# A linear-attention and gated-FFN layer on eight cores: other order of DMAs in the first tile, later residual rows, other order of the last output projections

## Chip, cores and metric

One Trainium2 chip, all 8 cores, each core running the same program on its own two of the sixteen sequences. The metric is the device time in microseconds of the slowest core; lower is better.

## What is computed

For each sequence x (2048 tokens of 1024 floats), after a layer norm `xn`:

```python
s = attn(xn)       # five mixed inputs x + (x_prev - x) * mu, products with r_w, k_w, v_w, g_w,
                   # a decay from tanh(.. @ w_w1.T) @ w_w2.T + w_b2, a recurrence over chunks of 32
                   # tokens with 4 heads (state 128 x 256), group norm per head, times silu(g), @ o_w.T
h = silu(xn @ wg.T) * (xn @ wu.T)        # wg, wu: 3072 x 1024, int32 weights / 127
g = silu(h @ wd.T)                       # wd: 1024 x 3072, int32 weights / 127
x = x + s * g
```

## The kernel before

**Tiles.** A core walks over its 4096 tokens in `N_MT` = 8 tiles of 512 tokens (`it` = 0 to 7); the tiles of one sequence hand the state `sb_S` and the last token on. A tile has `NST` = 4 rows of 128 tokens (`t`). All weights pass through SBUF in every tile, in slots: four for the gate and up weights (`sb_gu`, 24 steps `hc`, 512 KB each in bf16), four for a ring of eight attention weights (`sb_ring`: r, k, v0, v1, g0, g1, o0, o1, 1 MB each), and one half of the down weights in four groups `g` of six chunks (`sb_wd`, 768 KB each).

**Casts, stores and loads.** GpSimd's queue casts weights from their 4-byte originals (`w_gu`, `w_fd`, `w_g` and so on) to bf16 while they travel (`cast_gu`, `cast_ring`, `cast_wd`). At the last cast of a weight SyncE's queue stores the bf16 form to DRAM (`keep_gu`, `keep_ring`, `keep_wd`), and from the next tile on ScalarE's queue loads this form (`load_gu`, `load_ring`, `load_wd`). Down weights are cast in tile 0 alone, ring slots r and k in tiles 0 and 1, the others up to tile 3. A cast or load into a slot waits for the store of what lay in it (`k_wd`, `k_ring`, `k_gu`).

**A tile's stages.** TensorE's order is written out by hand (lines 1348 to 1501). Gate steps `gate_up(it, hc)` (16 matmuls each, lines 1180 to 1188) alternate with the mixing products, then r, k, v and g. Then for each row `t`: `out_and_kv` (recurrence), the transposes of the next tile's `xn`, `scores(t + 1)`, and two of eight down units. Unit `u` is row `u % 4` of half `u // 4`, so units 0 to 3 use the first half of the down weights and units 4 to 7 the second; pass t of this loop runs units 2t and 2t + 1, each as `down_first` (12 chunks, line 1300) and `down_second` (12 chunks, line 1311). The second half is loaded into the space of the first while units 3 and following run: group g as soon as unit 3 has used group g (`t_wd`, `t_D`). Transposes of the gated output (`og_transpose`, line 1325), its copy to `sb_ogT` by ScalarE (`copy_ogT`, line 687) and the output projection (`out_proj`, line 1339) follow two rows later; those of the third and fourth row (t = 2, 3) stand behind the last unit, between the first two gate steps of the next tile. The last tile has no next tile, so there they stand alone.

**The other engines.** VectorE's `output(it, t)` (line 1040) multiplies the projection by silu(down) and adds the residual row; `shift_and_xin0` (line 838) makes the first mixed input, and clears `sb_stash`, `sb_S` and `sb_Sb` at a sequence's start. ScalarE's `silu_down` (line 667) frees a down unit's bank.

**Order of the queues around the change.** A wait in a queue holds what is behind it. SyncE, tile 0: x rows for the next tile, stores of the first down half (line 388), residual rows one and two, x rows three and four, stores of o0 and o1, of the next tile's gate weights and r and k, stores of the second down half, residual rows three and four (after the last scores, line 332), output stores. GpSimd, tile 0: the first tile's casts by hand (lines 511 to 568), o0, o1, then the next tile's gate weights and ring slots r and k (line 602), and after the group norm of t = 1 the second down half (line 610). ScalarE: the second half is loaded at t = 1 and the first half for the next tile at t = 3 (line 794).

```python
                if t % 2 == 1:
                    for g in range(3):
                        load_wd(it + t // 2, 1 - t // 2, g)
                silu_down(it, 2 * t + 1)
                if t % 2 == 1:
                    load_wd(it + t // 2, 1 - t // 2, 3)
```

Of the kernel before, what the change touches and what calls it, by code (L numbers as in the profile page):

```python
# [102 lines left out]
N_MT = SPC * NMT  # L103
NGU = 4
# [38 lines left out]
def build_program():  # L143
# [165 lines left out]

    def d_unit(u):  # L310
        return (u % 4, u // 4)

    def sync_program(e):
# [52 lines left out]
        for it in range(N_MT):  # L366
            nxt = it + 1 < N_MT
            if it == 0:
                for hc in range(4):
                    keep_gu(0, hc)  # L370
            for hc in range(4, 10):
# [16 lines left out]
            for g in range(4):  # L388
                keep_wd(it, 0, g)
# [5 lines left out]
            keep_ring(it, 6)  # L395
            keep_ring(it, 7)
            if nxt:
                for hc in range(4):
                    keep_gu(it + 1, hc)
                keep_ring(it + 1, 0)  # L400
                keep_ring(it + 1, 1)
            for g in range(4):
                keep_wd(it, 1, g)
            load_res(it, 2)
            load_res(it, 3)
            for t in range(NST):
                store_out(it, t)
        for t in range(NST):
            e.wait_ge(d_out[t], 16 * N_MT)

    def pool_program(e):
# [157 lines left out]
        for it in range(N_MT):  # L569
# [28 lines left out]
            if nxt:  # L598
# [3 lines left out]
                for j in (0, 1):  # L602
                    cast_ring(it + 1, j, 0)
                    cast_ring(it + 1, j, 1)
            for t in range(NST):
# [3 lines left out]
                if t == 1:  # L609
                    for g in range(4):  # L610
                        cast_wd(it, 1, g, 0)
                        cast_wd(it, 1, g, 1)

    def scalar_program(e):
# [110 lines left out]
        for it in range(N_MT):  # L725
# [14 lines left out]
            for hc in range(6, 10):  # L740
                silu_gu(it, hc)
            if it:
# [43 lines left out]
            for t in range(NST):  # L786
# [11 lines left out]
                if t % 2 == 1:  # L798
                    load_wd(it + t // 2, 1 - t // 2, 3)
            copy_ogT(it, 2)  # L800
            if nxt:
                silu_gu(it + 1, 0)
            copy_ogT(it, 3)
            if nxt:
                silu_gu(it + 1, 1)

    def vector_program(e):
# [30 lines left out]
        def shift_and_xin0(it):  # L838
            if it % NMT == 0:
                if it:  # L840
                    e.wait_ge(t_ow, 4 * it)
# [198 lines left out]
        def output(it, t):  # L1040
            if t >= 2:
                e.drain()
            e.wait_ge(t_O, 4 * it + t + 1)
            e.wait_ge(a_D, 8 * it + 5 + t)
            for half in range(2):
                i = e.tensor_tensor(  # L1046
                    out=sg_sb[:, 512 * half:512 * half + 512],
                    in0=P_o[half][:],
# [12 lines left out]
        e.memset(sb_G64[:].rearrange("p b c -> p (b c)"), 1.0)  # L1061
        e.drain().then_inc(v_init, 1)
# [13 lines left out]
        ln_xnt(0, 0)  # L1076
        first_stat(2)
        ln_xnt(0, 1)
# [451 lines left out]
```

## Time and profile before

| | us |
|---|---|
| median of 3 runs (1811.79 to 1815.5) | 1813.17 |
| the profiled execution | 1834.1 |
| its span, slowest core (5) | 1832.5 |
| its span, fastest core (0) | 1803.2 |
| TensorE busy, core 5 | 1725.5 (94%) |
| VectorE, ScalarE, GpSimd busy | 1093.3, 476.9, 164.1 |

The profiled execution is another one than the timed ones and is taken on its slowest core. Busy time is time in which the engine executes; the waits of an engine are its idle stretches with what ended them. A queue's share is the time of its packets over 16 DMA engines and the span. MB count the bytes at the destination.

### The profile page before, as it was taken

To read this page: it belongs to the slowest core of one execution; us is meant where nothing else is said; L and a number is where in the kernel's file an instruction comes from. 1 tells how busy PE (TensorE), PEld (TensorE's weight loads), DVE (VectorE), ACT (ScalarE), POOL (GpSimd) and SP (SyncE) were. 2 spreads that over 40 slices of the span, in tenths; PEclk is the share of its full clock that TensorE was granted. 3 is DMA by queue.
4 is the path that set the end of the run, shared out by engine and by line. 5 is a ranking of instruction groups with operands and counts; after the bars stand their busy time and mean duration, and the time that the engine had idled before them with its cause. 6 is when DMAs were issued, how large, how long until landed. Compare 5 with 4: busy or idle time off the path is not lost.

```text
span 1832.5 us, 26740 instructions; the slowest of 8 cores (1803.2 to 1832.5 us)
## 1 busy us (share of the span) xinstructions
PE 1725.5 (94%) x9248; PEld 796.3 (43%) x9248; DVE 1093.3 (60%) x1887; ACT 476.9 (26%) x802; POOL 164.1 (9%) x354
## 2 busy tenths in 40 slices
PE   4999759999999999999999999999999999999997
PEld 2434424344444454444544444444454445444443
DVE  5554617465764847646664657656576485764654
ACT  0133201143211432125311332114321143212411
POOL 2211301101101011000100001000010001000000
PEclk9999869999999999999999999999999999999999
DMA  8999987997489954896545355543537454464231
GB/s 160 159 168 213 221 199 170 163 175 177 155 199 214 214 138 151 214 211 189 168 143 154 123 173 161 175 147 122 189 116 218 135 161 128 147 195 133 92 106 57
DMA packets 71506, 299.27 MB, mean 163 GB/s; under 512 B 8463, under 2 KB 8912, under 8 KB 64720
## 3 DMA queue, kind: packets, MB, share of 16 engines
q10 hardware_dynamic: 31680, 153.11, 26.9%
q0 software_dynamic: 19680, 66.76, 23.9%
q1 hardware_dynamic: 20016, 77.69, 12.8%
q8 instruction: 78, 1.28, 0.3%
q14 instruction: 52, 0.43, 0.1%
HBM read 320.25 MB, written 44.04 MB: 199 GB/s over the span
## 4 chain that ended last, share of the span: by engine, by line
PE 83%; DMA 11%; DVE 2%; issue 1%; DVEq 1%; ACT 1%; POOL 0%; ACTq 0%; SPq 0%; POOLq 0%
PE PB L1181 17%; PE PB L1186 16%; PE PB L1311 8%; PE PB L1300 7%; PE PB L1449 6%; PE PB L1473 6%; PE PB L1339 6%; DMA sb_wd<-kept_wd 4%; DMA sb_gu<-w_gu 4%; PE PB L1209 3%; PE PB L1392 3%; PE PB L1409 3%; DMA sb_wd<-w_fd 2%; PE PB L1359 1%; DMA sb_xin<-x 1%
## 5 line engine op out<-in xcount | busy, mean ns | idle before, releaser
L1181 PE MATMUL PB<-sb_xnT,sb_gu 128*128 128x512 bf16 x1536 | 369.0, 384 | 12.4 <-DMA sb_gu<-w_gu 9.7
L1186 PE MATMUL PB<-sb_xnT,sb_gu 128*128 128x512 bf16 x1536 | 364.8, 380 | 0.0
L814 DVE SCALAR_TENSOR_TENSOR sb_hall<-PB,sb_scr 128x512 bf16<-128x512 f32 x192 | 131.2, 687 | 333.2 <-ACT sb_scr L663 332.9
L663 ACT ACTIVATE sb_scr<-PB 128x512 bf16<-128x512 f32 x192 | 113.8, 597 | 613.7 <-PE PB L1186 607.5
L1181 PEld LDWEIGHTS PB<-sb_xnT,sb_gu 128*128 128x128 bf16 x1536 | 142.6, 98 | 210.7 <-issue 58.7
L1186 PEld LDWEIGHTS PB<-sb_xnT,sb_gu 128*128 128x128 bf16 x1536 | 151.0, 98 | 183.5 <-issue 4.1
L882 DVE SCALAR_TENSOR_TENSOR sb_xin<-PB,sb_xb,sb_dT 128x512 bf16<-128x512 f32 x320 | 217.3, 741 | 0.0
L1311 PE MATMUL PB<-sb_wd,sb_hall 128*128 128x512 bf16 x768 | 181.3, 385 | 30.2 <-DMA sb_wd<-kept_wd 21.9
L1300 PE MATMUL PB<-sb_wd,sb_hall 128*128 128x512 bf16 x768 | 180.3, 383 | 23.7 <-DMA sb_wd<-w_fd 21.0
L1311 PEld LDWEIGHTS PB<-sb_wd,sb_hall 128*128 128x128 bf16 x768 | 74.3, 98 | 122.3 <-issue 38.6
L672 ACT ACTIVATE sb_wc<-PB 128x512 bf16<-128x512 f32 x64 | 38.2, 597 | 338.8 <-PE PB L1311 338.8
L1339 PE MATMUL PB<-sb_ring,sb_ogT 128*128 128x512 bf16 x512 | 117.6, 383 | 3.7 <-ACT sb_ogT L687 3.3
L1300 PEld LDWEIGHTS PB<-sb_wd,sb_hall 128*128 128x128 bf16 x768 | 72.0, 98 | 107.6 <-issue 30.1
L1473 PE MATMUL PB<-sb_ring,sb_xin 128*128 128x512 bf16 x512 | 113.1, 379 | 0.0
L994 DVE SCALAR_TENSOR_TENSOR sb_S<-sb_S,sb_GS,PB 128x256 f32<-128x256 f32 x128 | 53.0, 476 | 99.5 <-PE PB L1288 99.5
L1449 PE MATMUL PB<-sb_ring,sb_xin 128*128 128x512 bf16 x512 | 111.8, 379 | 0.0
L888 DVE TENSOR_TENSOR sb_xin<-sb_xin,sb_xnT 128x2048 bf16<-128x2048 bf16 x80 | 98.0, 1225 | 7.3
L1046 DVE TENSOR_TENSOR sb_x<-PB,sb_wc 128x512 f32<-128x512 f32 x64 | 41.1, 684 | 76.5 <-PE PB L1339 74.9
L1025 DVE TENSOR_SCALAR sb_dT<-sb_dT,sb_mv,sb_rs 128x256 bf16<-128x256 f32 x128 | 44.2, 408 | 59.5 <-POOL sb_rs L508 59.5
L1339 PEld LDWEIGHTS PB<-sb_ring,sb_ogT 128*128 128x128 bf16 x512 | 50.2, 99 | 63.7 <-issue 6.9
L485 POOL TENSOR_SCALAR sb_lr<-sb_ls 128x1 f32<-128x1 f32 x28 | 12.0, 430 | 724.1 <-ACT sb_scr L654 724.0
L1449 PEld LDWEIGHTS PB<-sb_ring,sb_xin 128*128 128x128 bf16 x512 | 50.0, 98 | 60.5
(147 smaller groups left out, 1773.1 us busy)
## 6 DMA issues: line engine op xcount, KB each, us to landing
sb_gu<-kept_gu ACTq DMA_DIRECT2D x120, 512.0 KB, 4.1
sb_ring<-kept_ring ACTq DMA_DIRECT2D x44, 1024.0 KB, 7.4
sb_wd<-kept_wd ACTq DMA_DIRECT2D x56, 768.0 KB, 7.4
sb_gu<-w_gu POOLq DMA_DIRECT2D x72, 512.0 KB, 11.8
sb_xin<-x SPq DMA_DIRECT2D x48, 512.0 KB, 9.3
kept_gu<-sb_gu SPq DMA_DIRECT2D x24, 512.0 KB, 7.8
sb_ring<-w_g POOLq DMA_DIRECT2D x16, 512.0 KB, 11.9
kept_ring<-sb_ring SPq DMA_DIRECT2D x8, 1024.0 KB, 14.1
```

Source lines behind the costliest of these rows:

```text
L663: e.activation(out=sb_scr[:, p, :], in_=GB[p][:], func=AF.Silu, bias=0.0, scale=INV127).then_inc(a_silu, 1)
L814: e.scalar_tensor_tensor(out=sb_hall[:, hc, :], in0=UB[p][:], scalar=INV127, in1=sb_scr[:, p, :], op0=ALU.mult, op1=ALU.mult).then_inc(v_h, 1)
L882: e.scalar_tensor_tensor(out=sb_xin[:, p, c, :], in0=PM[j][:], scalar=sb_xb[:, n, c:c + 1], in1=sb_dT[:, c, :], op0=ALU.add, op1=ALU.mult) ...
L888: e.tensor_tensor(out=sb_xin[:, p, c0:c0 + 4, :], in0=sb_xin[:, p, c0:c0 + 4, :], in1=sb_xnT[:, c0:c0 + 4, :], op=ALU.add).then_inc(v_xin, 1)
L1181: e.matmul(GB[p][:], sb_gu[:, sl, 0, c, :], sb_xnT[:, c, :], start=(c == 0), stop=(c == NC - 1))
L1186: i = e.matmul(UB[p][:], sb_gu[:, sl, 1, c, :], sb_xnT[:, c, :], start=(c == 0), stop=(c == NC - 1))
L1209: i = e.matmul(PM[c % 4][:], sb_wx2[32 * n:32 * n + 32, 0, c * 128:(c + 1) * 128], sb_x5[32 * n:32 * n + 32, 0, :], start=True, stop=True, ...
L1300: i = e.matmul(PB[u % 2][:], sb_hall[:, hc, 128 * t:128 * t + 128], sb_wd[:, hc, :], start=(hc == 0), stop=False, skip_group_check=True)
L1311: i = e.matmul(PB[u % 2][:], sb_hall[:, hc, 128 * t:128 * t + 128], sb_wd[:, hc, :], start=False, stop=(hc == NHC - 1), skip_group_check=True)
L1339: i = e.matmul(P_o[half][:], sb_ogT[:, c, :], sb_ring[:, 2 + half, c, :], start=(c == 0), stop=(c == NC - 1), skip_group_check=True)
L1449: i = e.matmul(PM[t][:], sb_xin[:, 1, c, 128 * t:128 * t + 128], sb_ring[:, 2 + half, c, :], start=(c == 0), stop=(c == NC - 1))
L1473: i = e.matmul(PM[t][:], sb_xin[:, 0, c, 128 * t:128 * t + 128], sb_ring[:, half, c, :], start=(c == 0), stop=(c == NC - 1))
```

## The change

The order of SyncE's queue is changed (stores of ring slots r and k at the start of their tile, stores of down weights later, residual rows three and four after down unit 4, first output store ahead of the stores of o0 and o1). GpSimd casts ring slots r and k for tile 1 after the group norm of t = 2, and issues `w_x0` one cast later. ScalarE loads the next first down half at gate steps 6 to 9 of the tile that uses it. VectorE clears the state before it waits for the first rows, and normalises the second row before it takes statistics of the third. In the last tile the projection of the third row (t = 2) goes to banks 2 and 3 between the halves of down unit 7, the transposes of the third and fourth row stand around it, and the fourth row is projected, multiplied, added and stored in halves.

```diff
+LAST = N_MT - 1
+    def out_banks(it, t):
+        return PB[2:4] if it == LAST and t == 2 else P_o
 # load_res, t >= 2
-                e.wait_ge(t_mt, 4 * (it + 1))
+                e.wait_ge(t_D, 8 * it + 5)
 # store_out
+            if it == LAST and t == 3:
+                e.dma_start(out_d[s, ts, 0:512], res[t][:, 0:512]
+                            ).then_inc(d_out[t], 16)
+                e.wait_ge(v_out, 4 * it + t + 2)
+                e.dma_start(out_d[s, ts, 512:1024], res[t][:, 512:1024]
+                            ).then_inc(d_out[t], 16)
+                return
 # sync_program, start of a tile
+            keep_ring(it, 0)
+            keep_ring(it, 1)
...
-            for g in range(4):
-                keep_wd(it, 0, g)
             load_res(it, 0)
             load_res(it, 1)
             if nxt:
                 load_x(it + 1, 2)
                 load_x(it + 1, 3)
-            keep_ring(it, 6)
-            keep_ring(it, 7)
+            for g in range(4):
+                keep_wd(it, 0, g)
             if nxt:
                 for hc in range(4):
                     keep_gu(it + 1, hc)
-                keep_ring(it + 1, 0)
-                keep_ring(it + 1, 1)
+            load_res(it, 2)
+            load_res(it, 3)
+            store_out(it, 0)
+            keep_ring(it, 6)
+            keep_ring(it, 7)
             for g in range(4):
                 keep_wd(it, 1, g)
-            load_res(it, 2)
-            load_res(it, 3)
-            for t in range(NST):
+            for t in range(1, NST):
                 store_out(it, t)
 # pool_program
         ln_rstd(0, 0)
-        e.dma_start(sb_wx0[:], wdr["w_x0"]).then_inc(d_x0w, 16)
         ln_rstd(0, 1)
         cast_gu(0, 1)
+        e.dma_start(sb_wx0[:], wdr["w_x0"]).then_inc(d_x0w, 16)
...
                 for hc in range(0 if it else 2, 4):
                     cast_gu(it + 1, hc)
-                for j in (0, 1):
-                    cast_ring(it + 1, j, 0)
-                    cast_ring(it + 1, j, 1)
             for t in range(NST):
...
+                if t == 2 and nxt:
+                    for j in (0, 1):
+                        cast_ring(it + 1, j, 0)
+                        cast_ring(it + 1, j, 1)
 # scalar_program
             for hc in range(6, 10):
                 silu_gu(it, hc)
+                load_wd(it, 0, hc - 6)
...
                 if t < 3:
                     copy_ksT(it, t + 1)
-                if t % 2 == 1:
+                elif not nxt:
+                    copy_ogT(it, 2)
+                    copy_ogT(it, 3)
+                if t == 1:
                     for g in range(3):
-                        load_wd(it + t // 2, 1 - t // 2, g)
+                        load_wd(it, 1, g)
 # vector_program: the memsets of sb_stash, sb_S, sb_Sb for it == 0 stand ahead of v_init
         ln_xnt(0, 0)
+        ln_xnt(0, 1)
         first_stat(2)
-        ln_xnt(0, 1)
 # output, last tile, t == 3
+                e.wait_ge(a_D, 8 * it + 8)
+                e.wait_ge(d_res[t], 16 * (it + 1))
+                for half in range(2):
+                    hs = slice(512 * half, 512 * half + 512)
+                    e.wait_ge(t_O, 4 * it + t + 1 + half)
+                    e.tensor_tensor(out=sg_sb[:, hs], in0=po[half][:], in1=gff[...], op=ALU.mult)
+                    e.drain()
+                    e.tensor_tensor(out=res[t][:, hs], in0=res[t][:, hs],
+                                    in1=sg_sb[:, hs], op=ALU.add).then_inc(v_out, 1)
 # tensor_program, row loop
+                if t == 3 and not nxt:
+                    og_transpose(it, 2)
                 down_first(it, 2 * t + 1)
+                if t == 3 and not nxt:
+                    out_proj(it, 2)
+                    og_transpose(it, 3)
                 down_second(it, 2 * t + 1)
```

## Rows read from the trace of the kernel before

**Rows 1.** Head of the page.

```profile
span 1832.5 us, 26740 instructions; the slowest of 8 cores (1803.2 to 1832.5 us)
```

**Rows 2.** TensorE's waits, core 5: waited for, us in total, times, longest.

```profile
PE PB L1311 <- DMA sb_wd<-kept_wd: 21.9, 13, 2.8
PE PB L1300 <- DMA sb_wd<-w_fd: 21.0, 2, 18.5
...
PE PB L1311 <- DMA sb_wd<-w_fd: 8.2, 2, 6.1
```

**Rows 3.** TensorE's waits, core 0.

```profile
PE PB L1311 <- DMA sb_wd<-kept_wd: 9.0, 9, 1.7
```

**Rows 4.** Chain that ended last, first tile: start us, us, what.

```profile
217.94 41.43 DMA sb_wd<-w_fd
```

**Rows 5.** Page, DMA queues: packets, MB, share of 16 engines.

```profile
q10 hardware_dynamic: 31680, 153.11, 26.9%
q0 software_dynamic: 19680, 66.76, 23.9%
q1 hardware_dynamic: 20016, 77.69, 12.8%
```

**Rows 6.** Windows: us, busy PE PEld DVE ACT POOL, PEclk, DMA share, GB/s.

```profile
220.00:230.00 10.00, 1.33 (x28) 0.89 (x22) 7.84 (x22) 0.00 (x0) 2.16 (x3) 0.50 1.03 232
270.00:280.00 10.00, 10.00 (x66) 5.62 (x65) 6.30 (x18) 2.22 (x3) 0.26 (x2) 1.00 0.13 52
570.00:580.00 10.00, 10.00 (x46) 3.95 (x44) 7.07 (x11) 1.89 (x4) 0.86 (x2) 1.00 1.05 170
```

**Rows 7.** Timeline of the SyncE and GpSimd queues, tile 0: start us, us, what.

```profile
148.15 23.32 SPq L358 DMA_DIRECT2D kept_wd<-sb_wd  x4
...
188.12 14.27 SPq L325 DMA_DIRECT2D sb_xin<-x  x2
...
187.89 0.54 POOL L430 DMA_DIRECT2D sb_ring<-w_k  x1
...
213.98 0.69 POOL L467 DMA_DIRECT2D sb_wd<-w_fd  x1
```

**Rows 8.** Timeline of TensorE, tile 0 (in brackets: idle us before, what ended it).

```profile
166.19 2.18 PE L1181 MATMUL PB<-sb_xnT,sb_gu 128*128 128x512 bf16 x7 [3.74 <-DMA sb_gu<-w_gu]
...
239.81 2.72 PE L1300 MATMUL PB<-sb_wd,sb_hall 128*128 128x512 bf16 x6 [18.48 <-DMA sb_wd<-w_fd]
```

**Rows 9.** TensorE in tiles 1, 2; cast issued at 563.9; page, median gate load.

```profile
334.93 3.33 PE L1181 MATMUL PB<-sb_xnT,sb_gu 128*128 128x512 bf16 x8 [2.28 <-DMA sb_gu<-w_gu]
...
580.87 1.46 PE L1181 MATMUL PB<-sb_xnT,sb_gu 128*128 128x512 bf16 x6
...
sb_gu<-w_gu POOLq DMA_DIRECT2D x1, 512.0 KB, 15.2
...
sb_gu<-kept_gu ACTq DMA_DIRECT2D x120, 512.0 KB, 4.1
```

**Rows 10.** Chain, and timeline of SyncE, in tile 4's fourth stage.

```profile
1126.30 11.30 DMA sb_wd<-kept_wd
...
1129.22 0.33 SPq L333 DMA_DIRECT2D sb_ke<-x  x1
```

**Rows 11.** Timeline of VectorE and TensorE at the start.

```profile
27.83 0.91 DVE L843 MEMSET sb_S<- 128x1024 f32 x1 [0.16 <-issue]
...
37.27 1.89 PE L1356 MATMUL PB<-sb_xin,sb_wx 128*128 128x512 bf16 x8 [1.00 <-DVE sb_xin L859]
```

**Rows 12.** Timeline of TensorE and VectorE at the end.

```profile
1817.37 3.61 PE L1339 MATMUL PB<-sb_ring,sb_ogT 128*128 128x512 bf16 x16 [1.64 <-ACT sb_ogT L687]
...
1823.06 3.61 PE L1339 MATMUL PB<-sb_ring,sb_ogT 128*128 128x512 bf16 x16 [1.64 <-ACT sb_ogT L687]
...
1826.85 1.29 DVE L1046 TENSOR_TENSOR sb_x<-PB,sb_wc 128x512 f32<-128x512 f32 x2 [3.02 <-PE PB L1339]
1828.30 1.22 DVE L1054 TENSOR_TENSOR sb_k<-sb_k,sb_x 128x1024 f32<-128x1024 f32 x1 [0.16 <-issue]
```

More of the change, by code:

```diff
@@ L793, in scalar_program @@
                     copy_ksT(it, t + 1)
-                if t % 2 == 1:
+                elif not nxt:
+                    copy_ogT(it, 2)
+                    copy_ogT(it, 3)
+                if t == 1:
                     for g in range(3):
-                        load_wd(it + t // 2, 1 - t // 2, g)
+                        load_wd(it, 1, g)
                 silu_down(it, 2 * t + 1)
-                if t % 2 == 1:
-                    load_wd(it + t // 2, 1 - t // 2, 3)
-            copy_ogT(it, 2)
+                if t == 1:
+                    load_wd(it, 1, 3)
             if nxt:
+                copy_ogT(it, 2)
                 silu_gu(it + 1, 0)
-            copy_ogT(it, 3)
-            if nxt:
+                copy_ogT(it, 3)
                 silu_gu(it + 1, 1)
@@ L838, in shift_and_xin0 @@
         def shift_and_xin0(it):
-            if it % NMT == 0:
-                if it:
-                    e.wait_ge(t_ow, 4 * it)
+            if it and it % NMT == 0:
+                e.wait_ge(t_ow, 4 * it)
                 e.memset(sb_stash[:], 0.0)
@@ L1042, in output @@
                 e.drain()
+            po = out_banks(it, t)
+            if it == LAST and t == 3:
+                e.wait_ge(a_D, 8 * it + 8)
[3 more added lines that the diff above has]
+                    e.wait_ge(t_O, 4 * it + t + 1 + half)
+                    e.tensor_tensor(
+                        out=sg_sb[:, hs], in0=po[half][:],
+                        in1=gff[:, t * D + 512 * half:t * D + 512 * half + 512],
+                        op=ALU.mult)
+                    e.drain()
+                    e.tensor_tensor(out=res[t][:, hs], in0=res[t][:, hs],
+                                    in1=sg_sb[:, hs], op=ALU.add
+                                    ).then_inc(v_out, 1)
+                return
             e.wait_ge(t_O, 4 * it + t + 1)
@@ L1047, in output @@
                     out=sg_sb[:, 512 * half:512 * half + 512],
-                    in0=P_o[half][:],
+                    in0=po[half][:],
                     in1=gff[:, t * D + 512 * half:t * D + 512 * half + 512],
@@ L1061, in vector_program @@
         e.memset(sb_G64[:].rearrange("p b c -> p (b c)"), 1.0)
+        e.memset(sb_stash[:], 0.0)
+        e.memset(sb_S[:].rearrange("p h v -> p (h v)"), 0.0)
+        e.memset(sb_Sb[:].rearrange("p h v -> p (h v)"), 0.0)
         e.drain().then_inc(v_init, 1)
@@ L1321, in og_transpose @@
             e.wait_ge(v_S, 4 * it + s + 1)
-            if t == 3:
-                e.wait_ge(a_ogT, 4 * it + 3)
+            if t == 3 or (it == LAST and t == 2):
+                e.wait_ge(a_ogT, 4 * it + t)
             for c in range(NC):
@@ L1329, in out_proj @@
         def out_proj(it, t):
+            po = out_banks(it, t)
             e.wait_ge(a_ogT, 4 * it + t + 1)
             e.wait_ge(v_o, 4 * it + min(t + 2, 3) + 1)
-            if t == 3:
-                e.wait_ge(v_sg, 4 * it + 3)
-            elif t == 2:
+            if it == LAST and t == 2:
+                e.wait_ge(a_ksT, 4 * it + 4)
+                e.wait_ge(v_sel, 4 * it + 4)
+            elif it == LAST and t == 3:
                 e.wait_ge(v_sg, 4 * it + 2)
+            elif t >= 2:
+                e.wait_ge(v_sg, 4 * it + t)
             for half in range(2):
@@ L1338, in out_proj @@
                 for c in range(NC):
-                    i = e.matmul(P_o[half][:], sb_ogT[:, c, :],
+                    i = e.matmul(po[half][:], sb_ogT[:, c, :],
                                  sb_ring[:, 2 + half, c, :], start=(c == 0),
                                  stop=(c == NC - 1), skip_group_check=True)
+                if it == LAST and t == 3 and half == 0:
+                    i.then_inc(t_O, 1)
             i.then_inc(t_O, 1)
```

9 lines of the change are left out of this document (4 added, 5 removed).

## The prediction

> **What bounds the kernel now.** I read the page's head first: the profiled execution spans 1832.5 us on its slowest core, core 5, and 1803.2 us on its fastest [rows 1]. TensorE works for 94% of it, so only its idle time can be won. The waits of TensorE [rows 2] name that idle time. Two groups matter here: 21.0 + 8.2 us for casts of the down weights from `w_fd`, four waits that all lie in the first tile; 21.9 us for `kept_wd` loads, 13 waits over the later tiles. The chain of waits [rows 4] shows the first group as one transfer: the last cast of the second half of the down weights is issued at 217.94 and lands 41.4 us later, at 259.4. TensorE was ready for the first quarter of these weights at 239.81 - 18.48 = 221.3 [rows 8].
>
> Why it lands so late is in three more views. The queue rows [rows 5] give each queue's own rate: q0 (GpSimd's casts) moved 66.76 MB in 23.9% of 1832.5 us, 152 GB/s; q10 (ScalarE's loads) 310 GB/s; q1 (SyncE) 331 GB/s. By these a 512 KB cast costs 3.4 us of all 16 DMA engines, a 384 KB cast 2.6, a 768 KB load 2.5, a 1 MB store 3.2, a 512 KB residual row 1.6. The windows [rows 6] show the DMA full (1.03) at 220 to 230 with TensorE at half clock, and almost empty (0.13) at 270 to 280. The timeline [rows 7] shows that the casts of ring slots r and k, which only the next tile's r and k products need, are issued up to 187.89, ahead of the down casts (from 213.98) in the same queue.
>
> **The change part by part**, on core 5's profiled time, then on the median.
>
> *A, the start.* The three memsets (0.91 us for sb_S, as much for sb_Sb) leave VectorE's path to the first x0 product. TensorE waited 1.00 us there and before that worked on gate_up [rows 11], so 1.0 us is all they give. VectorE does them while it waits for the first x rows. The swapped first rows (`ln_xnt(0,1)`, `w_x0` behind a gate cast) end at the same landing of row four: 0. The displaced `w_x0` stands behind one more cast, 3.4 us, and is used at 37.27 at the earliest; both casts are issued in the first 15 us, so nobody waits.
>
> *B, gate cast 23 of the first tile.* It is waited for 3.74 us at 166.19 [rows 8]. Beside it SyncE's stores of the first down half run from 148.15 [rows 7], 2.4 us of DMA each. The change puts them behind the residual and x loads, near 202. Two of them, 4.7 us, leave the time of this cast: gain 3.7, bounds 0 and 3.7.
>
> *C, the second down half in the first tile.* The four ring casts (13.8 us of q0) go behind it. SyncE's o0 and o1 stores go behind the first output store; the four first-half stores come in their place, 9.5 us from 202. GpSimd's down casts wait for these stores, but by 214 they should have landed, since q0 holds nothing else then. Eight casts by 2.6 us and the time to landing (4.1 us for a 512 KB load whose transfer is 1.7 [rows 9], so 2.4) give 213.98 + 20.7 + 2.4 = 237.1, against 259.4: 22.3. The floor for the gain is the case that the stores hold q0 up for their whole 9.5 us: 13. The ceiling is the whole wait, 29.2. I take 23, since x row three, which GpSimd's queue waits for ahead of the casts, lands earlier too, and 1 us more because the matmuls behind it come back to full clock earlier (a group of six took 2.72 us behind the wait, where the clock of [rows 6] is half). The ring casts then run in the empty stretch near 250 to 280. Sum 24. Some 10 us of wait remain.
>
> *D, residual rows three and four.* They are issued at 1129.22, in the middle of the `kept_wd` loads whose last takes 11.3 us from 1126.30 [rows 10]. Now they wait for unit 4, which needs the last of these loads. Two rows are 3.2 us of DMA. As they land little later than the weights, about half of that was spent before them: I take 1.8 us a tile, 12.6 over seven tiles; bounds 0 and 21.9 [rows 2]. Their user is `output(it,2)`, three units later. Behind them in SyncE's in-order queue stands the first output store, ready only after the first out projection, which itself follows unit 4; so it is not held up. Of the Trainium skill, "DMA: Bandwidth & Descriptors" (Queues, rings and completion order) bears on this: each DMA engine takes turns between the queues that have work, a packet at a time. By that rule SyncE's rows take a full turn from the moment they are issued, and with 3.2 us a tile the sum would be 9.8 us larger on core 5. The issue times [rows 10] agree with turns being shared; no row shows how they are shared, so 1.8 stays.
>
> *E and F, the price.* The loads of the first down half for tile it+1 go from the end of tile it to gate steps 6 to 9 of tile it+1: 4 x 2.5 = 9.9 us of q10 at another place. Where they were, the gate weights had long landed. Where they go, tile 1 has waited for a cast already (2.28 us at 334.93) [rows 9], so it has no reserve. The loads also share with the stores of ring slots r and k (6.3 us), moved behind the output stores. Against this, the queue is emptier by the same 9.9 us before step 4. I take 4 us lost; bounds 0 and 10. In tile 2 the DMA is full (1.05 at 570 to 580 [rows 6]). The cast of step 13, issued at 563.9, lands 15.2 us later at 579.1, TensorE takes it at 580.87 [rows 9]: 1.8 us of reserve. Up to 9.9 - 1.8 = 8 can be lost; SyncE's stores carry a part: 5 taken. From tile 3 on a gate load takes 4.1 us [rows 9] and is issued three steps ahead. Six matmuls take 1.46 us [rows 9], so a step of 16 takes at least 3.4 and three 10.2: a 2.5 us neighbour is hidden, 0.
>
> *G, the end.* Two copies of ogT are waited for (1.64 us each) at 1817.37 and 1823.06 [rows 12]. The products of rows three and four now stand around the last down unit, whose matmuls cover both copies: 3.3. VectorE works in halves, so behind the last matmul there are one multiply (0.65) and half an add (0.6 to 0.7) and not 1.29 + 1.22: 1.3. The last store is half as large; with other small gaps 0.4. Sum 5, bounds 3 and 6. Row three's product moves to banks 2 and 3, whose last readers (the select and the copy of ksT for t = 3) stand before unit 6: no wait.
>
> Sum for core 5: 1.0 + 3.7 + 24 + 12.6 - 4 - 5 + 5 = 37.3, from 1834.1 us (span and 1.6 around it) to 1796.8. The median of the runs is 1813.17, 21 us under the profiled one, so its slowest core has shorter waits; core 0 shows 9.0 us where core 5 has 21.9 [rows 3]. C, B and G are alike on both cores; D I cut by the mean of the two, to 8.8. That leaves 33.5: **1780 us**.
>
> **The rivals.**
> (1) *The gates starve in tiles 1 and 2.* The moved loads meet a full DMA, and both tiles lose 8 to 10 us, with C at its floor of 13: gain 1 + 3.7 + 13 + 8.8 - 18 + 5 = 13.5, 1800 us. For it: the reserves of [rows 9]. Against: before step 4 there is less in the queues. The turns of the Trainium skill's page ("DMA: Bandwidth & Descriptors", the same section) speak for it as well: a cast that TensorE waits for gets no more turns than a load with time to spare. Chance 0.11.
> (2) *Slower.* ScalarE's queue is in order, so each gate load now stands behind a down load. If that starved the gates in all seven tiles by the full 9.9 us, 69 us would be lost against 42.5 won (the sum without E and F): 1813 + 27 = 1840. It decides from 6.1 us a tile. Against: 4.1 us to landing within 10.2 of lead leaves 6.1 for a 2.5 us neighbour. Chance 0.03.
> (3) *C does not come.* SyncE's in-order queue holds the first-half stores behind x row four, which waits for VectorE; if they land only at 230, GpSimd's down casts start there and land at 253.1: C is 6.3, the gain 1 + 3.7 + 6.3 + 8.8 - 9 + 5 = 15.8, 1797 us. Against: that x load was issued by 188.12 + 14.27 = 202.4 before [rows 7]. Chance 0.05.
> (4) *No price.* Tiles 1 and 2 hide the loads and C reaches 27: gain 45.5, 1768. It belongs to my forecast's range. Chance 0.16, and 0.65 for the forecast itself.
>
> **How the numbers follow.** A measurement of this kernel tells about 0.2%, 3.6 us, from no change. Faster by more: forecast, (4), (1) and (3), less a little for several mishaps together: 0.95. Slower by more 0.03, between 0.02. The range takes in (4) and most of C's and D's bounds on the fast side, 1764, and reaches short of the cases at 1797 and 1800 on the other, 1796.
>
> **What would show it.** C: the last `w_fd` landing near 232 to 237 after about 5 us of shift, and the w_fd waits down from 29 to about 10 us; (3) is right if the first down cast of the second half is issued after 220. B: no wait at gate cast 23. D: `kept_wd` waits at most half as long. E, F: new `sb_gu` waits at steps 8 to 13 of tiles 1 and 2, together near 9 us more than before; if they exceed 18, (1) is right, and if tiles 4 to 7 show any, (2). G: no wait for sb_ogT in the last 20 us. I am wrong if the time is above 1796, or if C gives under 15 us.

## The result, and the profile after

The changed kernel takes 1809.3 us (median of 20 runs) where the kernel before takes 1820.93 in as many: a ratio of 0.9914, 95% interval 0.9889 to 0.9938. Timed again later on another occasion (the run after_again, below) the ratio was 0.9883, 0.9844 to 0.9922. Eight of the changed kernel's 20 executions ran with a lower granted clock on one die (0.81 to 0.96) and took 1855 us or more, so the ratios are of the others and are not the quotient of the medians. So it is faster, by 16 to 21 us by the two ratios; the forecast was 1780 us, 33 us less than before, with a range from 1764 to 1796. The direction held and the size did not. Of the distance between 1780 and 1809.3, 7.8 us lies in the starting point: the forecast began at 1813.17, the median of three runs, where 20 runs give 1820.93.

The head of the page of the changed kernel, its rows of TensorE and of the DMA queues (packets, MB, share of 16 engines):

```profile
span 1799.9 us, 26572 instructions; the slowest of 8 cores (1783.3 to 1799.9 us)
...
PE 1711.7 (95%) x9073; PEld 795.4 (44%) x9248; DVE 1094.0 (61%) x1888; ACT 476.6 (26%) x802; POOL 164.2 (9%) x354
...
q10 hardware_dynamic: 31680, 153.11, 24.1%
q0 software_dynamic: 19680, 66.76, 23.4%
q1 hardware_dynamic: 20160, 77.69, 12.2%
```

The profiled executions differ more than the timed medians: 1834.1 us before, 1801.44 after. That of before [rows 1] is a long one among its runs (the 20 timed ones go from 1811.79 to 1837.18), so rows are not to be subtracted total from total, but stage by stage, over all eight cores. TensorE's waits in the profile after, core 4, the slowest (waited for, us in total, times, longest):

```profile
PE PB L1215 <- DMA sb_gu<-w_gu: 16.6, 7, 5.8
...
PE PB L1334 <- DMA sb_wd<-w_fd: 10.2, 2, 7.2
PE PB L1215 <- DVE sb_hall L830: 5.1, 2, 4.3
PE PB L1345 <- DMA sb_wd<-kept_wd: 4.8, 9, 1.2
...
PE PB L1345 <- DMA sb_wd<-w_fd: 3.8, 2, 2.7
```

Lines 1334, 1345 and 1215 are `down_first`, `down_second` and `gate_up`, lines 1300, 1311 and 1181 before. The waits for `w_fd` fell from 29.2 us [rows 2] to 14.0, those for `kept_wd` in `down_second` from 21.9 to 4.8. (Summed over both lines and as the mean of all eight cores they fell from 30.5 to 14.0 and from 15.2 to 4.7.) A new first row stands over them: 16.6 us for gate casts, on the mean of the cores 17.9 where it was 9.2. Of the 5.1 us of `sb_hall`, 4.3 are one wait in tile 2 of another kind, shown below.

**The stages.** Each tile is cut at two products that every core makes in the same place: the x0 product at its start, and the g product that ends its gate steps. "Front" is x0 to g, "back" is g to the next x0 (in the last tile, to the end). The table is worked out from the start times of these matmuls in the timeline; mean over the eight cores of one profiled execution each, in us. All kernels of the experiments stand in it, and the text comes back to it. The front of tiles 3 to 7 is 122.0 to 122.2 in every one.

```
kernel           to x0  front0 back0  front1  front2  backs 1-6  last back  span: mean, slowest
before            36.7  132.7  130.9  126.1   122.0    564.7       95.1     1817.9  1832.5
after             35.4  128.8  110.8  136.1   129.8    554.0       87.3     1792.0  1799.9
after_again       35.1  129.1  111.5  137.2   129.6    553.4       87.6     1793.2  1801.7
e1_loads_back     35.1  129.3  117.1  132.1   122.2    559.5       89.0     1794.0  1799.3
e2_loads_late     35.6  128.5  111.0  133.9   122.2    555.6       88.3     1785.0  1794.8
e3_rings_early    35.2  129.7  110.8  134.0   130.9    554.8       87.8     1793.0  1801.9
e4_only_res       36.2  133.7  130.4  125.6   122.1    555.2       92.9     1805.8  1813.6
e5_only_tail      36.1  132.3  130.5  126.7   122.2    559.1       88.1     1804.8  1813.2
e6_only_queues    36.4  128.8  123.9  125.7   122.2    560.6       94.4     1801.9  1813.5
e8_queues_late    36.5  128.6  113.8  125.4   122.2    556.3       94.2     1787.0  1793.9
e7_late_early     35.2  129.7  110.4  128.3   122.0    553.8       87.3     1776.5  1782.3
e7_again          34.9  129.3  111.3  128.5   122.6    552.3       87.3     1776.2  1783.4
```

Read the first two lines: every stage won, the back of tile 0 by 20 us, except two. The fronts of tiles 1 and 2 lost 10.0 and 7.8 us. That is where most of the missing gain went. On the mean of the cores TensorE's idle time in these two stretches grew by 7.4 and 5.6 us, nearly all at gate steps; the rest, 2.6 and 2.1, is longer busy time, since the matmuls behind a wait run slower (eight of them take 3.29 us at 315.95 below and 1.89 at 305.62; the granted clock was 0.53 from 316 to 319 us and 1.00 from 305.6 to 309). Its timeline in tile 1, core 4 (in brackets: idle us before, what ended it):

```profile
305.62 1.89 PE L1215 MATMUL PB<-sb_xnT,sb_gu 128*128 128x512 bf16 x8 [0.81 <-DVE sb_hall L830]
...
315.95 3.29 PE L1215 MATMUL PB<-sb_xnT,sb_gu 128*128 128x512 bf16 x8 [5.75 <-DMA sb_gu<-w_gu]
...
324.92 1.19 PE L1215 MATMUL PB<-sb_xnT,sb_gu 128*128 128x512 bf16 x4 [3.95 <-DMA sb_gu<-w_gu]
```

and in tile 2 on the same core:

```profile
558.34 3.27 PE L1215 MATMUL PB<-sb_xnT,sb_gu 128*128 128x512 bf16 x8 [1.89 <-DMA sb_gu<-w_gu]
566.10 1.89 PE L1215 MATMUL PB<-sb_xnT,sb_gu 128*128 128x512 bf16 x8 [1.80 <-DMA sb_gu<-w_gu]
573.97 2.34 PE L1215 MATMUL PB<-sb_xnT,sb_gu 128*128 128x512 bf16 x7 [4.25 <-DVE sb_hall L830]
```

The gaps are at steps 7, 8, 9 of tile 1 and 11, 12, 13 of tile 2. They do not all have one cause. The chain of waits (start us, us, what) runs through step 9 of tile 1:

```profile
281.74 0.33 SPq L349
...
282.17 0.40 SPq L362
...
282.65 1.05 SPq L362
...
283.80 20.01 DMA kept_gu<-sb_gu
...
304.33 20.34 DMA sb_gu<-w_gu
...
324.92 1.19 PE PB L1215 x4
```

From the bottom up: the matmuls of step 9 waited for their cast; that cast could be issued only at 304.33, because it overwrites the slot whose store (`kept_gu`) landed at 283.80 + 20.01 = 303.81; and this store was issued behind the last output store of tile 0 (line 349) and the two stores of ring slots r and k (line 362), which the change had moved right in front of it. Step 8 is another matter: its cast was issued at 295.59, when its slot was free, and took until 315.7 to land, beside the stores and, from 304.12 on, the first moved `kept_wd` load. So there were two suspects, the moved loads and the moved ring stores, and tile 1 alone could not tell which costs what.

The last gap of tile 2, 4.25 us at step 13, goes by yet another way. The chain there:

```profile
550.43 21.23 DMA kept_gu<-sb_gu
...
571.73 0.33 ACTq L635
...
572.21 0.61 ACT sb_scr L676
...
572.91 0.70 DVE sb_hall L830
...
573.97 2.34 PE PB L1215 x7
```

ScalarE's program has the load of gate weight 14 (line 635) behind the silu of step 10, and this load waits for the store of weight 10, which lay in the slot. The store took 21.2 us to land (9.1 in the kernel before on core 0 and 15.3 on core 4). The silu of step 11 stood behind that wait, VectorE's product behind the silu, and TensorE needed the bank for step 13. This wait (3.4 to 4.5 us) is on cores 0, 3, 4 and 6 alone: their front 2 is 132.6 to 133.6 us, that of the others 125.4 to 127.0. So nearly half of what tile 2 lost was not a late cast but ScalarE held by a slow store.

### The profile page after: what moved, and what is told of

The parts are those of the page before. It is cut to its first block, busy times and chain, and to the rows that moved or that the text cites. A ratio compares the mean times of both kernels' runs of the same rounds, so it can differ in the third digit from the quotient of the medians.

```text
span 1799.9 us, 26572 instructions; the slowest of 8 cores (1783.3 to 1799.9 us)
## 1 busy us (share of the span) xinstructions
PE 1711.7 (95%) x9073; PEld 795.4 (44%) x9248; DVE 1094.0 (61%) x1888; ACT 476.6 (26%) x802; POOL 164.2 (9%) x354
## 3 DMA queue, kind: packets, MB, share of 16 engines
q0 software_dynamic: 19680, 66.76, 23.4%
## 4 chain that ended last, share of the span: by engine, by line
PE 82%; DMA 12%; DVE 2%; issue 2%; DVEq 1%; ACT 1%; SPq 0%; POOL 0%; ACTq 0%; POOLq 0%
PE PB L1215 16%; PE PB L1220 16%; PE PB L1345 8%; PE PB L1334 7%; PE PB L1489 6%; PE PB L1513 6%; PE PB L1377 6%; DMA sb_gu<-w_gu 5%; PE PB L1449 3%; PE PB L1243 3%; DMA sb_wd<-kept_wd 3%; PE PB L1432 3%; DMA kept_gu<-sb_gu 2%; DMA sb_wd<-w_fd 1%; PE PB L1248 1%
## 5 line engine op out<-in xcount | busy, mean ns | idle before, releaser
L1215 PE MATMUL PB<-sb_xnT,sb_gu 128*128 128x512 bf16 x1489 | 365.1, 386 | 28.8 <-DMA sb_gu<-w_gu 16.6
L1334 PE MATMUL PB<-sb_wd,sb_hall 128*128 128x512 bf16 x730 | 173.5, 383 | 15.5 <-DMA sb_wd<-w_fd 10.2
L1345 PE MATMUL PB<-sb_wd,sb_hall 128*128 128x512 bf16 x752 | 179.0, 383 | 9.5 <-DMA sb_wd<-kept_wd 4.8
L685 ACT ACTIVATE sb_wc<-PB 128x512 bf16<-128x512 f32 x64 | 38.2, 597 | 315.6 <-PE PB L1345 315.6
L434 POOL DMA_DIRECT2D sb_gu<-w_gu x72 | 39.7, 552 | 400.2 <-PE PB L1220 354.7
```

The costliest lines, as they stand in the source:

```text
L1215: e.matmul(GB[p][:], sb_gu[:, sl, 0, c, :], sb_xnT[:, c, :], start=(c == 0), stop=(c == NC - 1))
L1334: i = e.matmul(PB[u % 2][:], sb_hall[:, hc, 128 * t:128 * t + 128], sb_wd[:, hc, :], start=(hc == 0), stop=False, skip_group_check=True)
L1345: i = e.matmul(PB[u % 2][:], sb_hall[:, hc, 128 * t:128 * t + 128], sb_wd[:, hc, :], start=False, stop=(hc == NHC - 1), skip_group_check=True)
```

## The experiments

All ratios are to runs of the kernel before on the same chip. That of e8 rests on two executions, those of e2 and e3 on three each, so these kernels are told apart by the stages and not by the ratios.

### Loads back, loads later, ring stores earlier: which of them starves the gates

**e1_loads_back**: the changed kernel with the loads of the next first down half where they were before.

```diff
             for hc in range(6, 10):
                 silu_gu(it, hc)
-                load_wd(it, 0, hc - 6)
...
-                if t == 1:
+                if t % 2 == 1:
                     for g in range(3):
-                        load_wd(it, 1, g)
+                        load_wd(it + t // 2, 1 - t // 2, g)
                 silu_down(it, 2 * t + 1)
-                if t == 1:
-                    load_wd(it, 1, 3)
+                if t % 2 == 1:
+                    load_wd(it + t // 2, 1 - t // 2, 3)
```

> The changed kernel with one part undone: the loads of the first down half for the next tile stand at t = 3 of the tile before again. In the changed kernel's profile the stretch from the x0 product to the g product is 135.8 us in tile 1 and 133.0 us in tile 2 on core 4 (before: 127.6 and 122.0 on core 5). Theory 1 (the moved loads starve the gate casts in tiles 1 and 2): both stretches fall by 7 to 11 us, to some 127 and 122, and the time is 0.7 to 1.0% under the changed kernel's ratio of 0.991, so 0.981 to 0.985 of before. Theory 2 (in tile 1 the stores of ring slots r and k, now at its start, are the cause): tile 2 falls to 122, tile 1 stays above 132; ratio 0.986. A wait of up to 5 us of ScalarE for the stores of the second down half may show at t = 3 of tile 0.

**e2_loads_late**: the changed kernel with these loads at gate steps 19 to 22, in tiles that have no shortage there.

```diff
-                load_wd(it, 0, hc - 6)
...
             for hc in range(19, 24):
                 silu_gu(it, hc)
+                if hc < 23:
+                    load_wd(it, 0, hc - 19)
```

> The changed kernel with the same four loads at gate steps 19 to 22 of the tile that uses them and not at steps 6 to 9; there the DMA was 0.25 to 0.83 busy in tile 1 of the kernel before. Theory 1: tile 1 and tile 2 stretches fall as without the move, to some 127 and 122 us, and no new wait comes at the first down unit, ratio 0.980 to 0.984. Theory 2: tile 1 stays above 132, ratio 0.986. If the late place collides with x rows and ring loads, waits for sb_wd at the first down unit show instead, 1 to 3 us a tile.

**e3_rings_early**: the changed kernel, loads as changed, but the stores of r and k of tile 1 at the end of tile 0's list instead of behind its output stores.

```diff
-            keep_ring(it, 0)
-            keep_ring(it, 1)
+            if it == 0:
+                keep_ring(it, 0)
+                keep_ring(it, 1)
...
             keep_ring(it, 6)
             keep_ring(it, 7)
+            if nxt:
+                keep_ring(it + 1, 0)
+                keep_ring(it + 1, 1)
```

> The changed kernel with one part undone: the stores of ring slots r and k are issued in tile 0 behind those of o0 and o1, not at the start of tile 1. Theory 2 (they delay the store of gate weight 5, and with it cast 9, and take 6.3 us of DMA from the casts of steps 6 to 8): the tile 1 stretch falls by 5 to 8 us, ratio 0.987. Theory 1: it falls by 0 to 3 us, since the loads at steps 6 to 9 remain; tile 2 stays as it is at 125 to 133; ratio 0.990 to 0.991.

Measured: e1 0.9872 (0.9837 to 0.9907), e2 0.9819 (0.9764 to 0.9873), e3 0.9881 (0.9838 to 0.9925).

**Tile 2 is settled**: its front is 122.2 in e1 and e2 and 130.9 in e3. The moved loads cost the whole 7.8 us there, by casts and by ScalarE's wait together, the ring stores nothing. **Tile 1 is not additive**: neither edit alone brings it back (132.1, 133.9, 134.0 against 136.1 to 137.2). Each suspect is enough to keep most of the loss. Core 5 of e2, where only the ring stores are left in the way, TensorE and then SyncE's queue:

```profile
298.47 1.89 PE L1216 MATMUL PB<-sb_xnT,sb_gu 128*128 128x512 bf16 x8 [0.65 <-DMA sb_gu<-w_gu]
305.95 3.16 PE L1216 MATMUL PB<-sb_xnT,sb_gu 128*128 128x512 bf16 x8 [2.91 <-DMA sb_gu<-w_gu]
314.05 1.89 PE L1216 MATMUL PB<-sb_xnT,sb_gu 128*128 128x512 bf16 x8 [2.24 <-DMA sb_gu<-w_gu]
321.76 3.15 PE L1216 MATMUL PB<-sb_xnT,sb_gu 128*128 128x512 bf16 x8 [4.10 <-DMA sb_gu<-w_gu]
```

```profile
279.28 0.33 SPq L349 DMA_DIRECT2D out<-sb_k  x1
279.71 1.36 SPq L362 DMA_DIRECT2D kept_ring<-sb_ring  x2
281.16 24.93 SPq L355 DMA_DIRECT2D kept_gu<-sb_gu  x2
```

Core 5 of e3, where only the loads are left:

```profile
309.07 1.89 PE L1219 MATMUL PB<-sb_xnT,sb_gu 128*128 128x512 bf16 x8 [0.75 <-DVE sb_hall L834]
320.51 3.57 PE L1219 MATMUL PB<-sb_xnT,sb_gu 128*128 128x512 bf16 x8 [7.83 <-DMA sb_gu<-w_gu]
```

The shapes differ. Ring stores give four small gaps at steps 6 to 9: the casts are slowed from the start (those of steps 7 and 8 take 17.2 and 20.7 us to land, 11.2 and 14.2 in e3), and cast 9 is issued late (303.06, after its `kept_gu` store landed 21.4 us after issue; in e3 that store takes 6.4 us and cast 9 goes out at 298.02). Loads give no more than 0.75 us before step 9 and one large gap there; its cast, issued on time, now takes 22.2 us. Both together overlap, since a late cast and a slow cast of the same step make one wait.

### Both at once

**e7_late_early**: both edits together, e2 and e3.

> Both undone at once: the loads of the first down half at gate steps 19 to 22, and the stores of ring slots r and k in tile 0. Each alone left the tile 1 stretch at 134 us (mean of cores), the changed kernel has 136, the kernel before 126. Theory 1+2 (two separate loads on a DMA that is full at steps 6 to 9; either alone is enough to starve the casts there): with both gone the stretch falls to 122 to 127 and the time to 0.972 to 0.978 of before. Rival (neither is the cause; tile 1 starts 25 us earlier against the rest of the DMA's work, for instance against its own chain of stored and recast gate weights): the stretch stays at 131 to 134, ratio 0.981 to 0.983.

Measured: **0.9737 (0.9694 to 0.9780)**, and once more beside the changed kernel on one chip:

> The changed kernel once more, to stand beside the next run on the same chip. If the ratio on record (0.991) is its own: 0.988 to 0.994. If the stages of the profiles are the whole story (20 us less than the kernel before on the mean of the cores): 0.987 to 0.990.

> The changed kernel with the loads at steps 19 to 22 and the stores of r and k for tile 1 at the end of tile 0, once more. By the stages of the profiles it is 15 us (0.9%) under the changed kernel, so 0.979 to 0.983 of the kernel before; by its first ratio (0.974) 30 us under it. Tile 1 from x0 to g 127 to 131 us, tile 2 122.0.

after_again 0.9883 (0.9844 to 0.9922); e7_again 0.9771 (0.9744 to 0.9798). This kernel beats both: over the changed one by 0.9771 / 0.9883 = 0.989, about 20 us, where the stages say 15.5 to 17. Its ratio came out a little below the 0.979 to 0.983 that the stages gave; the upper end of the interval, 0.9798, reaches into them. Front 1 is 128.3 and 128.5, just above the 122 to 127 first expected; front 2 is 122.0 and 122.6. So the two edits together give back 8.3 us of the 10.6 that tile 1 lost. Some 2.3 us remain against the kernels that leave tile 1 alone (125.4 to 126.7), and no run isolates their cause. Core 5 in tile 1:

```profile
307.96 1.89 PE L1220 MATMUL PB<-sb_xnT,sb_gu 128*128 128x512 bf16 x8 [0.39 <-DMA sb_gu<-w_gu]
...
315.40 3.57 PE L1220 MATMUL PB<-sb_xnT,sb_gu 128*128 128x512 bf16 x8 [3.83 <-DMA sb_gu<-w_gu]
```

and its chain there has no store left in it, a cast alone:

```profile
294.95 1.74 PE PB L1225 x8
...
297.28 17.88 DMA sb_gu<-w_gu
...
315.40 3.57 PE PB L1220 x8
```

The loads at steps 19 to 22 cost next to nothing in the table: front 2 is 122.0 to 122.6, and backs 1 to 6 are 553.8 and 552.3, as short as with the loads at steps 6 to 9.

### Parts of the change, alone, on the kernel before

**e4_only_res**: the kernel before with `load_res` for t >= 2 waiting for `t_D, 8 * it + 5`.

```diff
-                e.wait_ge(t_mt, 4 * (it + 1))
+                e.wait_ge(t_D, 8 * it + 5)
```

> The kernel before with one part of the change alone: residual rows three and four wait for down unit 4 and not for the last scores. My prediction's term D, 8.8 us on the median: ratio 0.995, kept_wd waits at the first unit of the second half down by half in each tile. Rival (the profiled execution of before was one with unusually long waits, and on a usual one the term is small): 2 to 4 us, ratio 0.998 to 0.999.

Measured 0.9958 (0.9928 to 0.9988): 7.7 us, with 2 to 13 in the interval. TensorE's waits on core 5 of this run, beside 21.9 us in the first group of [rows 2]:

```profile
PE PB L1311 <- DMA sb_wd<-kept_wd: 8.6, 12, 1.4
```

The stages correct this comparison. The kernels e5 and e6 keep the residual rows where they were, and their backs 1 to 6 sum to 559.1 and 560.6, not to the 564.7 of before. So about 5 us of what before's profile shows there belongs to that execution. Against the mean of the two, 559.9, the edit alone gives 4.7 us in six tiles, and 1.4 in the last (92.9 against 94.3, the mean of e6 and e8): 6.1. One run speaks against so much: e1 has this edit too, with the loads at t = 3 as here, and its backs 1 to 6 sum to 559.5, as in the kernels without it. The waits for `kept_wd` say the same (mean of the cores, us): 10.0 in e5, 11.9 in e6, 5.7 in e4, but 11.0 in e1. With one profiled execution of each the stages leave the size of this part open, from next to nothing to 6 us; the ratio says 2 to 13.

**e5_only_tail**: the kernel before with the changed last tile only, the same lines as in the change (`out_banks`, the copies, transposes and projections around unit 7, halves in `output` and `store_out`).

> The kernel before with the last tile's new order alone. My term G: 5 us, ratio 0.997, the last stretch of the profile some 5 us shorter (93 to 98 before), no wait of TensorE for sb_ogT in the last 20 us. Rival (the interleaved work is paid elsewhere): 0 to 2 us, ratio 0.999 to 1.000.

Measured 0.9937 (0.9905 to 0.9969), 11 us with 6 to 17; the last back is 88.1 against 94.3, that is 6.2. The ratio's centre is above what the stage shows and its interval touches it. In the changed kernel VectorE ends thus, core 4:

```profile
1794.34 0.69 DVE L1065 TENSOR_TENSOR sb_x<-PB,sb_wc 128x512 f32<-128x512 f32 x1 [2.02 <-PE PB L1377]
1795.11 0.69 DVE L1070 TENSOR_TENSOR sb_k<-sb_k,sb_x 128x512 f32<-128x512 f32 x1
1796.07 0.69 DVE L1065 TENSOR_TENSOR sb_x<-PB,sb_wc 128x512 f32<-128x512 f32 x1 [0.27 <-PE PB L1377]
1796.83 0.69 DVE L1070 TENSOR_TENSOR sb_k<-sb_k,sb_x 128x512 f32<-128x512 f32 x1
```

Two halves of 0.69 us behind the last matmul where [rows 12] have 1.29 + 1.22; and no wait for `sb_ogT` is left among TensorE's.

**e6_only_queues**: the kernel before with the order of SyncE's and GpSimd's queues in tile 0 only (r and k for tile 1 are stored in tile 0, as in e3); loads, residual wait, start and tail as before.

```diff
             load_res(it, 0)
             load_res(it, 1)
...
+            for g in range(4):
+                keep_wd(it, 0, g)
             if nxt:
                 for hc in range(4):
                     keep_gu(it + 1, hc)
+            load_res(it, 2)
+            load_res(it, 3)
+            store_out(it, 0)
+            keep_ring(it, 6)
+            keep_ring(it, 7)
+            if nxt:
                 keep_ring(it + 1, 0)
                 keep_ring(it + 1, 1)
...
+                if t == 2 and nxt:
+                    for j in (0, 1):
+                        cast_ring(it + 1, j, 0)
+                        cast_ring(it + 1, j, 1)
```

> The kernel before with the order of the SyncE and GpSimd queues of tile 0 alone (down stores later, r and k casts behind the second down half, o stores behind the first output store, r and k stores behind them in tile 0); loads of the first down half at t = 3, start, residual wait and tail as before. My terms B and C: the stretch from the g product to the next tile falls from 131 by 14 to 20 us (ScalarE may wait some 5 us for the stores at t = 3), tile 1 stays near 126: ratio 0.988 to 0.990. Rival: without the late load of the first half tile 1 is as in the run with these loads back, 132, ratio 0.992 to 0.993.

Measured 0.9925 (0.9885 to 0.9964), where 0.988 to 0.990 was expected. Front 1 and 2 are unharmed (125.7, 122.2). But the back of tile 0 won only 7 us and not the 14 to 20 expected, though the waits for `w_fd` fell to 17 us (core 7: 13.0 + 3.8). The chain of core 0 says where the rest went:

```profile
252.67 22.03 DMA kept_wd<-sb_wd
...
274.77 0.33 ACTq L644
...
275.19 0.61 ACT sb_wc L675
...
275.94 3.57 PE PB L1189 x8
```

SyncE's stores of the second down half now go out later. ScalarE's in-order queue waits at t = 3 for those stores before it may load the next first half over them (`kept_wd` store of 22.0 us, then the issue on line 644), and behind this wait stands `silu_down`, whose copy into `sb_wc` frees the bank for the gate step. TensorE waited 10.0 us for it on this core, 4.2 to 7.4 on the others. e1, the other kernel with the earlier casts and the loads at t = 3, shows the same: 0.7 to 6.3 us of this wait, and a back 0 of 117.1 where the changed kernel has 110.8.

**e8_queues_late**: e6 with the loads at gate steps 19 to 22 and nothing else changed.

> The kernel before with the order of SyncE's and GpSimd's queues in tile 0, and with the loads of the next first down half issued at gate steps 19 to 22 of the tile that uses them; start, residual rows and tail as before. Theory: the earlier down casts can't pay in full while ScalarE's in-order queue waits in row t = 3 for the stores of the second down half, behind which its copy for gate step 0 of tile 1 stands; with the loads out of that place the wait for sb_wc (4 to 10 us on the cores of the run with the queue order alone) is gone, the stretch from tile 0's g product to tile 1's x0 product takes 110 to 113 us on every core instead of 124, tile 1 from x0 to g takes 126 to 131 us, tile 2 122; the time is 0.975 to 0.985 of the kernel before. Rival: the residual rows that this kernel still issues beside the casts cost the rest, so that the stretch stays above 117 us with no ScalarE wait in it.

Measured 0.9844 (0.9791 to 0.9898). Back 0 falls from 123.9 to 113.8, no `sb_wc` wait is left, front 1 is 125.4. (The cores lie at 112.5 to 114.5, above the 110 to 113 expected; the residual rows beside the casts may be the rest.) So moving the loads out of t = 3 is not a side issue of this change: it is what lets the earlier casts pay. Backs 1 to 6 are also 4.3 us shorter (560.6 to 556.3). The place they were moved to was the fault.

## Why the prediction was right in direction and wrong in size

By its own terms, with the baseline for each stage taken from the kernels that leave that stage alone:

- **A, the start**: 1.0 expected. To x0: 36.4 (mean of before, e4, e5, e6, e8) to 35.3 (mean of both runs of after). Right, 1.1.
- **B, gate cast 23**: 3.7 expected. Front 0 went from 132.9 to 129.0, and e6, e8 show it with the queue order alone. Right, 3.9; step 23 still waits, but 0.7 us on the mean of the cores where it waited 3.5 (core 4: 0.67).
- **C, the second down half**: 24 expected, 13 to 29 as bounds. Back 0 went from 130.6 to 111.2: 19.4. The mechanism was right. The chain of core 4 has the store and the cast behind it:

```profile
199.93 13.40 DMA kept_wd<-sb_wd
...
214.37 20.85 DMA sb_wd<-w_fd
```

  The last landing, 214.37 + 20.85 = 235.2, is inside the 232 to 237 that was named, but TensorE came to it 5 us earlier by A and B, so by the prediction's own working (237.1 less 5) it is 3 us late. The sentence "by 214 they should have landed" came true (the last store landed at 213.3), but the sum added A and B in full beside C, and for that the stores and the casts had to move forward by the same 5 us; the last landing came only 1.9 us before 237.1. GpSimd's timeline on core 4 (in brackets: idle us before, what ended it):

```profile
206.41 0.65 POOL L479 DMA_DIRECT2D sb_wd<-w_fd  x1 [0.79 <-PE PB L1334]
...
211.52 0.53 POOL L479 DMA_DIRECT2D sb_wd<-w_fd  x1 [2.75 <-DMA kept_wd<-sb_wd]
...
213.85 0.53 POOL L479 DMA_DIRECT2D sb_wd<-w_fd  x1 [1.27 <-DMA kept_wd<-sb_wd]
```

  The first cast went out at 206.4, 7.6 us earlier than before, while the four stores were still on their way. But the casts got next to nothing until the stores were done: from 206.4 to 211.0 us SyncE's queue q1 had 97.5% of the 16 engines and q0 no packet, with four casts issued; from 213.5 to 222 q0 had 103%. So from the first issue to the last landing it took 235.2 - 206.4 = 28.8 us, where 23.1 had been worked out (20.7 + 2.4), and 23.1 fits if counted from 212, when q0 began to move. A part of the "floor" case of the prediction, in which the stores hold q0 up, is what came. Of the wait, 14 us remained and not 10; and the matmuls behind each wait ran at half clock as they did before. The windows of core 4 (us, busy PE PEld DVE ACT POOL, PEclk, DMA share, GB/s):

```profile
220.00:230.00 10.00, 5.81 (x20) 2.23 (x20) 4.18 (x8) 1.02 (x1) 2.25 (x4) 0.50 1.03 156
```

- **D, residual rows**: 8.8 on the median, 12.6 on core 5. In the changed kernel backs 1 to 6 and the last give 6.2 + 1.4 = 7.6 (559.9 to 553.7, and e4's last back); alone it gives 6.1 by the stages and 7.7 (2 to 13) by the ratio. The sum is near the forecast, but it is not D's alone: by e8 the moved loads shorten the same stretches by 3.6 us without it (559.9 to 556.3), which leaves 2.6 and the last tile's 1.4, and e1 shows no gain from D in these stretches. So that 7.6 lies near 8.8 is in part luck; the prediction gave the moved loads no gain here. The correction from core 5 to the median was needed, and should have been larger: the profiled execution was a bad one in just these waits. The turn rule of the Trainium skill, "DMA: Bandwidth & Descriptors" (Queues, rings and completion order), would have added 9.8 us to the sum for core 5; the runs do not bear that out.
- **E and F, the price**: 4 and 5 expected, bounds 10 and 8. Measured 136.7 - 126.1 = 10.6 and 129.7 - 122.1 = 7.6, 18.2 in all. **This is the step that failed**, a term mis-sized by 9 us, with tile 1 past its bound and tile 2 close to it. Two sentences of it were wrong. "The queue is emptier by the same 9.9 us before step 4", and so something is given back: it isn't. With ring stores and all else alike, front 1 is 125.7 with the loads at t = 3 (e6) and 125.4 with them at steps 19 to 22 (e8): an emptier queue before step 4 gives 0.3 us. And in tile 2 "SyncE's stores carry a part": on four cores it was the reverse, since the slowed `kept_gu` store held ScalarE, and by it TensorE, for 3.4 to 4.5 us. In tile 1 the ring stores were counted as DMA time only (6.3 us to share). They cost that (the 5.8 us of waits at steps 6 to 8 in e2 are slow casts), and besides it their place in SyncE's in-order queue, ahead of a `kept_gu` store which holds a slot for which GpSimd's cast waits (the 4.1 us at step 9). The prediction priced these stores by their bytes and did not ask what stands behind them. It also left out the clock: in the changed kernel's profile 4.7 of the 17.8 us lost are matmuls that ran slower behind the waits, a term that it counted in C (1 us gained) and not here.
- **G, the end**: 5 expected, 3 to 6 as bounds. By the stages 5.4 in the changed kernel (92.9 to 87.5) and 6.2 alone. Right.

Sum by stages: 1.1 + 3.9 + 19.4 + 7.6 - 10.6 - 7.6 + 5.4 = 19.2, against 33.5 expected, and 16 to 21 by the ratios. The distance of 14.3 is E and F with 9.2, C with 4.6, D with 1.2, less 0.7 that A, B and G gave above what was expected. Rival (1), given 0.11, was half right: its E and F of 18 is what came, its C of 13 is not; 18 with the other terms of the forecast would have made 1789. The prediction named a sign for it ("if they exceed 18, (1) is right"); read as waits alone the sign did not show, since TensorE's idle time in the two fronts grew by 13 us, and only with the slower matmuls are there 18. It had the 1.8 us reserve of tile 2 and none for tile 1 in [rows 9]: both spoke for the bound, and values near the middle were taken. Rival (3), a late start of the casts behind SyncE, was wrong: they were issued from 206.4 and moved from 212. Rival (2) was wrong: fronts 3 to 7 are 122.0 to 122.2 throughout.

The same page of the Trainium skill was cited for rival (1), by which a cast that TensorE waits for gets no more turns than a load with time to spare. The sizes agree with it: with one 768 KB load after another beside them the gate casts of steps 9 and 10 take 22.2 and 23.0 us from issue to landing (core 5 of e3), without them 17.9 and 15.5 (core 5 of e7). Tile 0 speaks against an equal share: there q0 had no packet from 206.4 to 211.0 us with four casts issued, and q1 had 97.5%, while a cast issued into an idle DMA (at 268.62) had q0 at 38.2% over its first 2 us. Why the casts got no turn there is shown by no run.

What was argued and not run: the start (A) alone, the place of the ring stores apart from their DMA time, the 2.3 us that front 1 keeps in e7, and the share of clock in C's missing 4.6 us. In e6 and e8 the wait for `w_fd` is about 3 us longer than in the changed kernel with the same stores and casts; the residual rows beside them are the likely cause, and no run isolates it in that tile.

## What to carry to other kernels

Before a store is moved in an in-order queue, follow the chain behind it: which store is next, which slot does it free, and who is waiting to fill that slot. Its bytes are only a part of its price. The same holds for a load issued by an engine that also computes: what stands behind it in the program waits too. A transfer set down where the DMA is full can cost nearly all its bytes when the work beside it has little reserve (here 7.6 us in tile 2 for 9.9 us of loads), so take the bound there and look for a later stretch instead; here thirteen steps later cost next to nothing. And test the parts in pairs: the queue order alone gave 7 us in tile 0, with the loads out of ScalarE's way 17, and neither of two fixes for tile 1 did much without the other.

## What the runs showed of the hardware that was not expected

The in-order queues coupled engines through slots: behind SyncE's ring stores a gate store took 20 us to land (6.4 without them, e3), and so GpSimd's cast went out 5 us later (303.06 against 298.02), and so TensorE waited. A slow store held ScalarE in the same way, for the second down half in e6 (10.0 us of TensorE on core 0) and for a gate weight in tile 2 (4.25 us on core 4). While SyncE's stores ran, casts already issued did not move at all (97.5% of the engines for q1, no packet of q0, from 206.4 to 211.0 us). The casts' queue kept its rate: 66.76 MB in 23.4% of 1799.9 us is 159 GB/s, where [rows 5] give 152. And one profiled execution can differ from its fellows by some 5 us in one kind of wait (564.7 against 559 to 561 in backs 1 to 6, with nothing changed there), which is as much as a term of this forecast.
